# Every second layer-0 tile of a two-layer block: the down product as three rounded products

## What is computed

```python
g = jnp.einsum('th,ehi->tei', x, Wg)
u = jnp.einsum('th,ehi->tei', x, Wu)
h = jax.nn.silu(g) * u * coef[:, :, None]
moe_out = jnp.einsum('tei,eih->th', h, Wd)
shared = jax.nn.silu(x @ SWg) * (x @ SWu) @ SWd
```

## Time and profile before

| | |
|---|---|
| three runs | 1780.97, 1779.66, 1776.04 us; median 1779.66 |
| profiled execution, span from the first to the last instruction | 1724.1 us |
| profiled execution, own time | not marked among the runs; taken as the median, so 55.6 us lie around the span |
| granted TensorE clock, mean | 0.989 of full speed |

### The profile page before, as it was taken

How to read it: one execution, slowest core, us unless ns; L and a number is a source line. 1 busy time by engine, 2 the same in 40 slices (tenths; PEclk the granted TensorE clock), 3 DMA queues, 4 the chain that set the end, 5 groups by cost and what they waited for, 6 DMA issues and landing times.

```text
span 1724.1 us, 24432 instructions
## 1 busy us (share of the span) xinstructions
PE 1679.7 (97%) x7020; PEld 1188.6 (69%) x7020; DVE 1350.6 (78%) x3866; ACT 812.6 (47%) x1456; POOL 609.5 (35%) x656
## 2 busy tenths in 40 slices
PE   5999999999999999999999999999999999999995
PEld 4667777777777777777777777777777766667773
DVE  5878888888888787979797979787888776565558
ACT  4535453636363545454544445454545343554431
POOL 3311242424242324233333232332323233567770
PEclk8999999999999999999999999999999999999998
DMA  8949474646373747373737373645546445577758
GB/s 211 201 104 256 100 187 105 178 109 181 99 181 101 182 103 194 97 200 86 202 84 192 85 189 90 174 106 135 144 106 167 99 109 154 191 266 266 237 173 312
DMA packets 172339, 273.89 MB, mean 159 GB/s; under 512 B 14312, under 2 KB 57320, under 8 KB 171952
## 3 DMA queue, kind: packets, MB, share of 16 engines
q1 hardware_dynamic: 163632, 254.63, 56.1%
q0 software_dynamic: 8576, 17.70, 3.2%
HBM read 202.15 MB, written 65.93 MB: 155 GB/s over the span
## 4 chain that ended last, share of the span: by engine, by line
PE 94%; DVE 2%; ACT 1%; issue 1%; DMA 1%; POOL 0%; SPq 0%; POOLq 0%; DVEq 0%; ACTq 0%
PE ps_y L709 26%; PE ps_gate L660 8%; PE ps_gate L661 8%; PE ps_gate L662 8%; PE ps_up L662 8%; PE ps_up L660 8%; PE ps_up L661 8%; PE ps_y L735 4%; PE ps_side L675 3%; PE ps_side L758 1%; PE ps_side L852 1%; PE ps_side L835 1%; PE ps_side L794 1%; PE ps_side L819 1%; PE ps_side L660 1%; PE ps_side L661 1%
## 5 line engine op out<-in xcount | busy, mean ns | idle before, releaser
L918 DVE TENSOR_TENSOR silu_h<-ps_up,silu_h 128x512 f32<-128x512 f32 x618 | 424.0, 686 | 295.3 <-ACT silu_h L1325 243.3
L1325 ACT ACTIVATE silu_h<-ps_gate 128x512 f32<-128x512 f32 x618 | 367.6, 598 | 567.4 <-PE ps_gate L662 565.1
L709 PE MATMUL ps_y<-silu_h,w_dn 128*128 128x512 f32 x1056 | 542.7, 595 | 3.0 <-DVE silu_h L912 3.0
L912 DVE TENSOR_TENSOR silu_h<-coef_b,silu_h 128x512 f32<-128x512 f32 x528 | 386.8, 732 | 13.0 <-DMA coef_b<-coef_kept 9.2
L660 PE MATMUL ps_gate<-xnT,w_gu 128*128 128x512 f32 x528 | 342.7, 649 | 0.0
L709 PEld LDWEIGHTS ps_y<-silu_h,w_dn 128*128 128x128 f32 x1056 | 199.7, 189 | 53.7 <-issue 7.7
L660 PE MATMUL ps_up<-xnT,w_gu 128*128 128x512 f32 x528 | 207.9, 394 | 4.6 <-DVE silu_h L918 4.6
L661 PE MATMUL ps_gate<-xnT,w_gu 128*128 128x512 f32 x528 | 209.4, 397 | 0.0
L662 PE MATMUL ps_gate<-xnT,w_gu 128*128 128x512 f32 x528 | 208.9, 396 | 0.0
L662 PE MATMUL ps_up<-xnT,w_gu 128*128 128x512 f32 x528 | 208.0, 394 | 0.0
L661 PE MATMUL ps_up<-xnT,w_gu 128*128 128x512 f32 x528 | 206.8, 392 | 0.0
(11 more groups left out here) (267 smaller groups left out, 2454.8 us busy)
## 6 DMA issues: line engine op xcount, KB each, us to landing
coef_b<-coef_kept SPq DMA_DIRECT2D x254, 512.0 KB, 6.8
slots_x<-empty SPq DMA_DIRECT2D x15, 2080.0 KB, 12.7
w_block<-w_kept SPq DMA_DIRECT2D x45, 512.0 KB, 3.9
xs<-slots_x SPq DMA_DIRECT2D x37, 260.0 KB, 3.8
y_back<-y_kept SPq DMA_DIRECT2D x15, 512.0 KB, 7.0
w_down<-in_ffn_w SPq DMA_DIRECT2D x45, 128.0 KB, 3.7
w_raw<-in_ffn_w SPq DMA_DIRECT2D x33, 128.0 KB, 7.9
xres<-in_x SPq DMA_DIRECT2D x16, 256.0 KB, 3.1
```

Source lines behind the costliest of these rows:

```text
L709: eng.matmul(ps_y[:, :], w_dn[:, j], silu_h[:, g % HBUFS], start=j == 0, stop=last).then_inc(pe_down)
L912: eng.tensor_tensor(silu_h[:, s], coef_b[:, q % COEF_RING, k], silu_h[:, s], ALU.mult).then_inc(dve_h)
L918: eng.tensor_tensor(silu_h[:, s], ps_up[g % 2][:, :], silu_h[:, s], ALU.mult).then_inc(dve_h1)
L1325: eng.activation(silu_h[:, s], ps_gate[g % 2][:, :], ACT.Silu).then_inc(act_silu)
```

## The change

In tiles with odd j, the down product is made like gate and up: three products of rounded operands. The high part of the input, h_hi (a ring of two), is made by ScalarE as a rounding copy of silu_h; the rest, h_lo (one buffer), by GpSimd as silu_h - h_hi. Both stand at the head of step j + 2 of their engine's list (SPLIT_LATE = 2), on ScalarE ahead of silu. Two products read h_hi; then TensorE waits for h_lo. The down weights of odd tiles are loaded with gate and up, and split with them in chunk 0 (128x384 instead of 128x256). Even tiles and the shared expert keep the full-precision product.

With it come: another layout of the weights (w_two, w_last, w_dn of 17 tiles in three loads); SP's and ScalarE's waits in the last chunk for down instead of up products (8, 12, 22 instead of 9, 15, 27); the sends of chunk 13 at steps 10 to 17; and 2048 bytes instead of the default for the descriptors of GpSimd's DMAs.

```diff
-DOWN_PART = 11
+DOWN_PART = 8
-TILES_UNDER_XS, TILES_UNDER_XST, TILES_UNDER_WEIGHTS = 9, 15, 27
+TILES_UNDER_XS, TILES_UNDER_XST, TILES_UNDER_WEIGHTS = 8, 12, 22
+HI_BUFS, LO_BUFS, SPLIT_LATE = 2, 1, 2
+ROUTE1_THEN = [(at, what) for at, what in ROUTE1 if not what.startswith("send")] + [(43 + n, f"send{n}") for n in range(TOP1 * ROWS)]
...
-        plan[g] += [(what, c - 2) for at, what in ROUTE1 if at == j + TILES0 and c > 1]
+        plan[g] += [(what, c - 2) for at, what in (ROUTE1 if c < SPARSE else ROUTE1_THEN) if at == j + TILES0 and c > 1]
...
+        h_hi = sb("h_hi", [HI_BUFS, CHUNK], FP32R)
+        h_lo = sb("h_lo", [LO_BUFS, CHUNK], FP32R)
...
-        w_gu = sb("w_gu", [TILES0, 2, 2, P], FP32R, within=ffn0)
-        w_dn = sb("w_dn", [TILES0, P], within=ffn0)
+        w_two = sb("w_two", [PAIRS0 // 2, 5 * 2, P], FP32R, within=ffn0)
+        w_last = sb("w_last", [2 * 2, P], FP32R, within=ffn0)
+        w_dn = sb("w_dn", [PAIRS0 // 2 + 1, P], within=ffn0)
...
-            eng.wait_ge(pe_up, (CHUNKS - 1) * TILES0 + TILES_UNDER_XS)
+            eng.wait_ge(pe_down, (CHUNKS - 1) * TILES0 + TILES_UNDER_XS)
...
+                if odd(g):
+                    n, w = odd_before(g), weights0(j)[:, 2]
+                    hi, lo = h_hi[:, n % HI_BUFS], h_lo[:, n % LO_BUFS]
+                    eng.wait_ge(act_hhi, n + 1)
+                    eng.matmul(ps_y[:, :], w[:, 0], hi, start=False, stop=False)
+                    eng.matmul(ps_y[:, :], w[:, 1], hi, start=False, stop=False)
+                    eng.wait_ge(pool_hlo, n + 1)
+                    eng.matmul(ps_y[:, :], w[:, 0], lo, start=False, stop=False).then_inc(pe_down)
+                    return
...
+            def h_round(g):
+                n = odd_before(g)
+                eng.wait_ge(dve_h, scaled_before(g) + 1)
+                if n >= HI_BUFS:
+                    eng.wait_ge(pe_down, odd_at(n - HI_BUFS) + 1)
+                eng.copy(h_hi[:, n % HI_BUFS], silu_h[:, g % HBUFS]).then_inc(act_hhi)
...
+                if odd(g - SPLIT_LATE):
+                    h_round(g - SPLIT_LATE)
                 if TILES_FIRST <= g < TILES + UNITS1:
                     silu(g)
...
+            def h_rest(g):
+                n = odd_before(g)
+                eng.wait_ge(act_hhi, n + 1)
+                if n >= LO_BUFS:
+                    eng.wait_ge(pe_down, odd_at(n - LO_BUFS) + 1)
+                eng.tensor_tensor(h_lo[:, n % LO_BUFS], silu_h[:, g % HBUFS], f32(h_hi[:, n % HI_BUFS]), ALU.subtract).then_inc(pool_hlo)
...
+                if odd(g - SPLIT_LATE):
+                    h_rest(g - SPLIT_LATE)
                 for what, key in plan[g]:
                     step(what, key, g)
...
-    nc = bacc.Bacc("TRN2", target_bir_lowering=False, num_devices=1)
+    nc = bacc.Bacc("TRN2", target_bir_lowering=False, num_devices=1, dynamic_dma_scratch_size=2048)
```

More of the change, by code:

```diff
@@ L284, in build_program @@
         early = ExitStack()
-        w_raw = sb("w_raw", [STAGES_W, 2, P], within=early)
+        w_raw = sb("w_raw", [STAGES_W, 3, P], within=early)
         raw1 = sb("raw1", [4 * P + EXPERTS1], within=early)
@@ L331, in build_program @@
         common_in, raw0_in, kvr_in, c0_in, w_out_in, bias0_in = (sem(n) for n in ("common_in", "raw0_in", "kvr_in", "c0_in", "w_out_in", "bias0_in"))
-        w_dn_in = [sem(f"w_dn_in{n}") for n in range(TILES0 // DOWN_PART)]
+        w_dn_in = [sem(f"w_dn_in{n}") for n in range(PAIRS0 // 2 // DOWN_PART + 1)]
         raw1_in, causal_in, f1_in, b1_in = (sem(n) for n in ("raw1_in", "causal_in", "f1_in", "b1_in"))
@@ L427, in scaled_before, with odd, odd_before, odd_at @@
             return c * PAIRS0 + j
+        def odd(g):
+            return 0 <= g < TILES and g % TILES0 % 2 == 1
+        def odd_before(g):
+            c, j = tile_of(g)
+            return c * (PAIRS0 // 2) + j // 2
+        def odd_at(n):
+            c, k = divmod(n, PAIRS0 // 2)
+            return c * TILES0 + 2 * k + 1
+        def weights0(j):
+            if j == TILES0 - 1:
+                parts = w_last[:, :, :]
+            else:
+                parts = w_two[:, j // 2, 4:10] if j % 2 else w_two[:, j // 2, 0:4]
+            return parts.rearrange("p (a b) d -> p a b d", b=2)
+        def raw_of(n):
+            return w_raw[:, n % STAGES_W, 0:2 + n % 2]
         def dense(g):
@@ L473, in sync @@
             load_x(1)
-            for n in range(TILES0 // DOWN_PART):
+            even = ffn_w[0:PAIRS0, :, 2 * P:].rearrange("(n t) p d -> t p n d", t=2)[0]
+            for n in range(PAIRS0 // 2 // DOWN_PART):
                 these = slice(n * DOWN_PART, (n + 1) * DOWN_PART)
-                eng.dma_start(w_dn[:, these], ffn_w[these, :, 2 * P:].rearrange("n p d -> p n d")).then_inc(w_dn_in[n], 16)
+                eng.dma_start(w_dn[:, these], even[:, these]).then_inc(w_dn_in[n], 16)
+            eng.dma_start(w_dn[:, PAIRS0 // 2], ffn_w[PAIRS0, :, 2 * P:]).then_inc(w_dn_in[-1], 16)
             def load_rest(n):
@@ L703, in last_products @@
                     eng.matmul(ps_y[:, :], w_out[:, :], mix_a[:, :], start=False, stop=False).then_inc(pe_mix)
+                if odd(g):
[7 more added lines that the diff above has]
+                    return
                 h_ready(g)
-                if c == 0 and j % DOWN_PART == 0:
-                    eng.wait_ge(w_dn_in[j // DOWN_PART], 16)
+                if c == 0 and j // 2 % DOWN_PART == 0:
+                    eng.wait_ge(w_dn_in[j // 2 // DOWN_PART], 16)
                 if j == 0 and c > 0:
                     eng.wait_ge(act_y, c)
-                eng.matmul(ps_y[:, :], w_dn[:, j], silu_h[:, g % HBUFS], start=j == 0, stop=last).then_inc(pe_down)
+                eng.matmul(ps_y[:, :], w_dn[:, j // 2], silu_h[:, g % HBUFS], start=j == 0, stop=last).then_inc(pe_down)
             def first_of_unit(u):
```

17 lines of the change are left out of this document (8 added, 9 removed).

## The result

The changed kernel takes 1857.93 us (median of 4 runs, 1855.35 to 1860.67), the kernel before beside it 1778.49 (1776.04 to 1780.97): a ratio of 1.0456, 95% interval 1.0439 to 1.0473. It is 79 us slower; 1793 us had been predicted, 1825 was the upper end.

What follows compares the result with a forecast made beforehand. TensorE was taken as the bound, busy 1679.7 of 1724.1 us. Products -49, lateness of the rest +68 and last chunk -6 gave +13 on 1779.7, so 1793 us, range 1750 to 1825.

Steps and rivals of the forecast that it cites:

- A: TensorE waits 60 to 90 us in third products for GpSimd, outweighing cheaper products: 1785 to 1815 us, chance 0.43.
- ScalarE's rounding: 256 copies on ScalarE, 159 us in all, hidden in 900 us idle; only their place ahead of silu delays others.
- VectorE beside GpSimd: Rests on GpSimd block VectorE's coefficient products, 0.70 us each; taken as nothing, upper end 30 us.
- The products: Odd down products on TensorE become three rounded ones, 0.19 us less for each of 256 tiles: -49 us.
- Lateness of the rest: h_lo on GpSimd comes late for TensorE, mainly at tiles 5, 9, 13, 15, 27: +68 us, between 29 and about 100.
- The clock: Waits of 1.9 us at tile 9 could lower TensorE's clock: 24 us over 14 chunks, not in the sum.
- rival C: VectorE becomes the bound around tiles 10 to 23 through collisions with GpSimd: +43 us, 1823 us, chance 0.15.
- The last chunk: Chunk 13's sends moved to steps 10 to 17 spare waits and slow clock there: -6 us, ends 0 and 8.
- The scratch: Descriptor scratch cut to 2048 bytes: nothing; 21 us at the upper end if sends wait for room.
- The 55.6 us around the span: The profiled span lies 55.6 us under the median of three runs; kept unchanged and added to the forecast time.
- B: The kernel ends faster, h_lo late only by the unpushed 29 us: -26 us, 1754 us, chance 0.30.

Runs made afterwards that it cites:

- the memsets: Changed kernel, third product reading h_hi without waiting, two memsets of h_lo replacing GpSimd's subtraction: 1710.61 us, 0.9909 of the kernel before.
- the lag runs: Changed kernel, down product four steps behind gate and up instead of three: 1810.84 us (one h_hi buffer), 1806.76 (two), 1831.06 (two, rounding behind silu).

## Why the prediction was wrong in size

The direction and the mechanism of A were right: slower, TensorE waiting in the third product for GpSimd's rest. What failed are the terms set at nothing: ScalarE's rounding and VectorE beside GpSimd. The sum was -49 + 68 - 6 = +13 for the profiled execution; by the runs, in the order of the table, it is -42 + 61 - 5 + 68 = +82, where the last 68 stand for ScalarE 19, memsets 12 and subtractions 37. By the changed kernel's own trace (1811.4 us, 86 more than the kernel before) the same time divides otherwise: -47 for the products and the last chunk, +95 of late third products, at most 19 at half clock, and 20 of all else. Step by step:

- **The products**, -49: measured -42. TensorE gets 0.178 us a tile in middle chunks, not 0.19 (the prediction's own costs, 0.87 less 0.69, give 0.18).
- **Lateness of the rest**, +68: 95 by the starts of the third products, 61 by the run without the wait, in which other delays come up instead. That the term looks right by its size against 61 is in part luck. The list by tiles was good: tile 9 24.1 us (26 predicted), tile 5 18.0 (16), chunk 0 4.3 (4). Tile 27 was 18.0 (7 predicted): its rest starts when an addition of the messages ends, as foreseen, but takes 1.72 us and not 1.28; it starts while VectorE is in a product with the coefficients, and is longer by about what that still runs (rows below). Tile 15 was 23.7 (15 for it and tile 13), up to 3.5 us in one chunk.
- **ScalarE's rounding**, "the work itself is hidden": this failed, 19 us. Its push was looked for at the silus of tiles 5 and 9 and not around the two table loads, whose window was never read.
- **GpSimd's being held**, no term: 12 us by the memsets, of which a part is VectorE's (16 us busier).
- **VectorE beside GpSimd**, "With half of them colliding (2.5 us) it fits, and I take nothing": this is the step that failed most, 37 us by the runs in which TensorE doesn't wait, above even its upper end of 30. The mechanism was seen, but it was counted on one instruction in a window of 40 us, "seven rests and seven coefficient products". 256 rests meet whatever VectorE then does, and two 16-column instructions lost 1.9 us at once. In the changed kernel itself most of these 37 and of ScalarE's 19 lies hidden behind the waits for h_lo, as the steps of chunk 8 show.
- **The clock**, no term for the middle chunks, but 24 us in rival C for waits at tile 9: it does fall, though behind tile 15 (2.0 to 3.5 us late), and once behind tile 27 (1.3), and never behind tile 9 (1.7 to 1.8); by the estimate above for 6 to 9 us. It is a part of the 61.
- **The last chunk**, -6: -4.9. **The scratch**, 0: 0. Both held.
- **The 55.6 us around the span**: wrong. They are a difference between chips, in layer 1. It did no harm to the difference, since the ratio is the same on both.

Tile 27 in chunk 8 of the changed kernel, timeline of GpSimd, VectorE and TensorE:

```profile
864.70 1.29 POOL L1639 TENSOR_TENSOR msg<-msg 128x512 f32<-128x512 f32 x1 [1.83 <-ACT msg L1520]
...
865.57 0.96 DVE L953 TENSOR_TENSOR silu_h<-coef_b,silu_h 128x512 f32<-128x512 f32 x1
...
865.93 1.72 POOL L1646 TENSOR_TENSOR h_lo<-silu_h,h_hi 128x512 fp32r<-128x512 f32 x1
...
867.71 0.61 PE L743 MATMUL ps_y<-h_lo,w_two 128*128 128x512 f32 x1 [1.18 <-POOL h_lo L1646]
```

Rival C (VectorE the bound, 1823 us) is not what the changed kernel shows: C's sign, TensorE's up product waiting for VectorE in the middle of each chunk, makes 9.8 us in all (4.6 in the kernel before). It comes up once the wait for h_lo is taken away, 30.6 us. So A and C don't exclude each other, as the chances had it: C's cost lies under A's. B's condition, waits under 55 us, was not met. Even without TensorE's waiting for h_lo the change is 21 us slower: more time for the rest would not have saved it, as the lag runs show.

Two things stay open: how the 12 and 37 us would divide with a memset exactly as long as the rest, and what the 20 us of all else in the changed kernel's layer 0 consist of.

## What to carry to other kernels

Work moved to an idle GpSimd can be paid for on VectorE. Look at every VectorE instruction of a stretch that works in SBUF, the small ones too, and not at one costly kind: here each 1.36 us subtraction took 0.33 to 0.6 us of VectorE. When several terms of a change can happen at once, add them in the upper end; but a delay can hide another one, so a run with one part taken out gives that part's price with the others in place, and not its share of the loss. And for each engine that gets work, read the fullest stretch of the chunk, not its mean idle time.

## What the runs showed of the hardware

Two GpSimd subtractions back to back (0.75 and 1.27 us) held two VectorE instructions of 16 columns, 0.36 us together, for 2.27 us. Those of 128x512 (1.36 us in the mean) added 84 us to VectorE's busy time, 0.33 us each over 256. Begun 0.7 us later against VectorE's product with up, they added 0.6 us each ((1510.1 - 1351.7) / 256), the busy time of the run without a rest subtracted in both. Memsets of the same tile, 0.53 us, added 16 us over 512. VectorE's product with up, one input in PSUM, took 0.68 to 0.70 us beside them as alone. A wait of TensorE of 1.87 us was followed by 3.4 us at half clock, in which products of 128x512 started 0.43 us apart. A load of ScalarE's function table took 1.28 us, and the exponentials of a chunk's attention need two of them between two silus.
